# Second attention of a transformer block: scores in four row groups and four banks, softmax in pieces of 616, projection one pair later

## What is computed

```python
q = proj(query, Wq, bq); k = proj(key, Wk, bk); v = proj(value, Wv, bv)     # 16 heads of 16 channels
scores = jnp.einsum('bhqd,bhkd->bhqk', q, k) * scale[None, :, None, None]
scores = scores + _rel_bias(bias_table, tq, tk)[None]
attn = jax.nn.softmax(scores, axis=-1)
out = jnp.einsum('bhqk,bhkd->bhqd', attn, v)
out = out.transpose(0, 2, 1, 3).reshape(b, tq, DIM) @ Wo + bo
x = x + jnp.tanh(g_xattn[1]) * out
```

## Time and profile before

| | us |
|---|---|
| median of 3 runs | 486.8 (486.63 to 487.26) |
| profiled execution, first to last instruction | 485.3 |
| second attention, about | 218 to 361 |
| TensorE busy over the span | 434.0 (89%) |
| VectorE, ScalarE, POOL busy | 334.4, 258.2, 128.3 |
| mean granted TensorE clock, share of full | 0.959 |

### The profile page before, as it was taken

How to read it: one execution, slowest core, us unless ns; L and a number is a source line. 1 busy time by engine, 2 the same in 40 slices (tenths; PEclk the granted TensorE clock), 3 DMA queues, 4 the chain that set the end, 5 groups by cost and what they waited for, 6 DMA issues and landing times.

```text
span 485.3 us, 7506 instructions
## 1 busy us (share of the span) xinstructions
PE 434.0 (89%) x2308; PEld 300.7 (62%) x2309; DVE 334.4 (69%) x732; ACT 258.2 (53%) x453; POOL 128.3 (26%) x143
## 2 busy tenths in 40 slices
PE   8998999999975079999899999999896799999993
PEld 7878544444451078788576577766575467676762
DVE  4999973489998999655667776766827355555562
ACT  3563655599989934323656566655651343332310
POOL 6423262000002504210870000100011754543222
PEclk9999999999985579999999999999998999999998
DMA  8900000000010040000991000000008321221000
GB/s 255 249 3 0 3 2 0 0 0 0 0 58 1 0 105 1 0 0 18 386 407 57 1 1 1 2 0 0 1 20 243 87 78 49 71 51 48 14 30 1
DMA packets 27421, 27.20 MB, mean 56 GB/s; under 512 B 11611, under 2 KB 23586, under 8 KB 27139
## 3 DMA queue, kind: packets, MB, share of 16 engines
q1 hardware_dynamic: 25187, 21.73, 14.5%
q0 software_dynamic: 2208, 5.14, 3.6%
HBM read 22.63 MB, written 5.15 MB: 57 GB/s over the span
## 4 chain that ended last, share of the span: by engine, by line
PE 60%; DVE 17%; issue 3%; ACT 3%; DMA 3%; POOL 2%; DVEq 1%; ACTq 0%; POOLq 0%
PE bank L1661 49%; PE bank L1947 4%; PE bank L1705 3%; DVE big_g L478 2%; DVE big_g L1387 2%; DVE amP L1361 2%; PE bank L2143 2%; DMA token_rows<-x_rows 2%; ACT big_u L760 2%; PE bank L1965 2%; DVE amZ L1297 1%; DVE amU L1303 1%; DVE mx L1482 1%; DVE big_g L1483 1%; PE bank L1973 1%
## 5 line engine op out<-in xcount | busy, mean ns | idle before, releaser
L1661 PE MATMUL bank<-yT,ffn_w 128*128 (+1 forms) x192 | 83.0, 593 | 0.0
L760 ACT ACTIVATE big_u<-bank 77x512 f32<-77x512 f32 (+3 forms) x102 | 56.3, 583 | 34.8 <-PE bank L1947 24.3
L1661 PEld LDWEIGHTS bank<-yT,ffn_w 128*128 128x128 f32 x192 | 36.2, 190 | 44.8 <-issue 43.1
L1661 PE MATMUL bank<-ffn_w,big_u 128*128 128x256 f32 x192 | 42.6, 380 | 0.8 <-ACT big_u L760 0.8
L984 ACT ACTIVATE big_g<-big_g 128x308 f32<-128x308 f32 x64 | 29.0, 456 | 26.1 <-DVE big_g L1483 25.6
L1661 PE MATMUL bank<-k_blockdiag,big_g 128*128 128x308 f32 x128 | 40.2, 430 | 2.5 <-DVE big_g L1483 2.2
L1661 PE MATMUL bank<-big_g,yT 128*128 x92 | 41.8, 595 | 0.6 <-ACT yT L760 0.6
L1059 ACT ACTIVATE yT<-yT 128x512 f32<-128x512 f32 x23 | 14.5, 630 | 52.1 <-DVE yT L1616 52.1
L1661 PE MATMUL bank<-big_u,yT 128*128 x184 | 41.8, 380 | 0.2 <-DVE yT L1630 0.2
L1661 PEld LDWEIGHTS bank<-ffn_w,big_u 128*128 128x128 f32 x192 | 36.2, 190 | 6.0 <-ACT big_u L760 0.9
L1661 PEld LDWEIGHTS bank<-big_u,yT 128*128 128x128 f32 x184 | 34.1, 190 | 5.0 <-issue 0.9
(11 more groups left out here) (293 smaller groups left out, 845.8 us busy)
## 6 DMA issues: line engine op xcount, KB each, us to landing
big_g<-in_L_ffn_W SPq DMA_DIRECT2D x1, 4096.0 KB, 13.5
big_u<-in_L_ffn_W SPq DMA_DIRECT2D x1, 4096.0 KB, 24.5
...
```

Of the source, the lines that this page charges most:

```text
L760: act.activation(out_, in_, ACT.Copy, **k).then_inc(done, 1)
L1661: return pe.matmul(out_, lhsT=lhsT, rhs=rhs, start=first, stop=last)
```

## The change

Each pair is now treated in two halves of eight heads (ci = 0, 1) in place of four quarters.

- Scores (`fill`): for each tile and each group r of 32 rows of `qT` and `KBD` one matmul of 32 rows by 154 columns (the two heads whose channels these rows are), into bank r. A fill is eight matmuls: four row groups for two tiles, side by side in banks 0 to 3 (`quad`). A fill waits until both tiles of the fill before have been read.
- Softmax (`unit`): maximum and subtraction over four banks at once, 616 elements, per tile and half; the exponential in pieces of 616 too.
- The weights' transposes of one tile use banks 6 and 7 in turn; heads are two blocks of eight matmuls into bank 5, the transposes back into banks 5 and 6, queries and projection both in bank 4.
- The projection of pair t - 4, no longer of t - 2, is issued during pair t, and so are its residual and moments. Two projections (pairs 12 and 14) are left for the tail.
- The last four down tiles, and the late layer norm tiles, get other banks and places around pair 0.
- All hardware loops of the stage are written out. `oT` gets memory of its own, and `pT` another order of its quarters (`PLACES`).

```diff
@@ -26,6 +26,10 @@
 HQ = 4
...
+HC = H // CH
+HCK = HC * KEYS
+RG = 4
+RK = HCK // RG
...
 FJ = F // P
@@ -244,8 +248,9 @@
         def sem(name):
             return ctx.enter_context(nc.semaphore(name))
-        bank = [ctx.enter_context(nc.psum_tensor(f"bank{i}", [P, 512], F32)) for i in range(8)]
-        pb = [b[:, :] for b in bank]
+        quad = ctx.enter_context(nc.psum_tensor("quad", [P, 4, 512], F32))
+        bank = [ctx.enter_context(nc.psum_tensor(f"bank{i}", [P, 512], F32)) for i in range(4, 8)]
+        pb = [quad[:, i, :] for i in range(4)] + [b[:, :] for b in bank]
         rows_d = nc.dram_tensor("token_rows", [NT * P, ROW], F32).ap()
@@ -393,9 +398,9 @@
...
-        oT = part(TMP, 0, [P, NQ, 2 * P])
+        oT = sb("heads_out", [P, NQ, 2 * P])
...
-        mx = sb("mx", [P, 2, HQ])
+        mx = sb("mx", [P, 2, HC])
...
@@ -453,8 +458,8 @@
         ob = part(YW, 3584, [P, 2, D])
...
+        LAST = NT - 2
+        PLACES = (0, 2, 1, 3)
         def position(t):
@@ -967,55 +971,54 @@
...
+            def weightsT(t, ci, u):
+                for k in range(2):
+                    o = PLACES[2 * ci + k] * HQ
+                    copy(pT[:, o:o + HQ, u * P:(u + 1) * P], pb[6 + k][0:KEYS, :].rearrange("k (h p) -> k h p", h=HQ),
+                         s.pT_ps, 2 * (2 * t + 2 * ci + u) + k + 1, s.pT_sb)
+            def heads_out(t, ci):
+                copy(oT[:, 2 * ci:2 * ci + 2, :], pb[5].rearrange("p (a n) -> p a n", a=2), s.oT_ps, t + ci + 1, s.oT_sb)
             def attended(t):
                 act.wait_ge(s.attT_ps, t + 2)
...
+                act.activation(attT, pb[5 if t == LAST else 4].rearrange("p (a n) -> p a n", a=2), ACT.Copy).then_inc(s.attT_sb, 2)
+            def exponents(t, ci, u):
+                e8 = e_[:, u, ci * HCK:(ci + 1) * HCK]
+                act.wait_ge(s.e_sub, 2 * t + 2 * ci + u + 1)
+                act.activation(e8, e8, ACT.Exp).then_inc(s.e_exp, 1)
+            def pair(t):
+                if t:
+                    weightsT(t - 2, 1, 0)
+                    if t >= 4:
+                        attended(t - 4)
                     else:
...
+                        y3_out_late(NQB - 1, 0)
+                    weightsT(t - 2, 1, 1)
+                    if t < 4:
+                        y3_out_late(NQB - 1, 1)
+                exponents(t, 0, 0)
+                if t == 0:
+                    y3_out_late(NQB - 2, 0)
+                    y3_out_late(NQB - 2, 1)
+                exponents(t, 0, 1)
+                if t:
+                    heads_out(t - 2, 1)
+                weightsT(t, 0, 0)
+                weightsT(t, 0, 1)
+                exponents(t, 1, 0)
+                if t < LAST:
+                    queries(t + 2)
+                exponents(t, 1, 1)
+                heads_out(t, 0)
+            for t in range(0, NT, 2):
+                pair(t)
+            weightsT(LAST, 1, 0)
+            attended(LAST - 2)
+            weightsT(LAST, 1, 1)
             def y4T_out(k):
@@ -1026,10 +1029,11 @@
                 copy(lT[:, g, :], pb[(0, 4)[g % 2]][:, 0:P], s.lT_ps, g + 1, s.lT_sb)
             y4T_out(0)
...
+            y4T_out(1)
+            heads_out(LAST, 1)
+            for k in range(2, 5):
                 y4T_out(k)
...
+            attended(LAST)
             y4T_out(5)
             logits_out(0)
             logits_out(1)
@@ -1445,102 +1449,94 @@
             def head_out(t, u):
                 dve.wait_ge(s.o_ps, t + u + 1)
...
+                o = pb[u if t == LAST else 5 + u][:, 0:H * VE].rearrange("p (h d) -> p h d", d=VE)
                 c.link(dve.reciprocal(rd[:, u, :], o[:, :, HD]))
                 dve.tensor_tensor(att[:, u, :].rearrange("p (h d) -> p h d", d=HD), o[:, :, 0:HD],
                                   rd[:, u, :].unsqueeze(2).to_broadcast([P, H, HD]), ALU.mult).then_inc(s.att_sb, 1)
...
+            def residual(t, u):
                 dve.wait_ge(s.wo_ps, t + 2)
...
+                x = X[:, tile_at(t) + u, 0:D]
+                dve.tensor_tensor(x, pb[5 if t == LAST else 4][:, u * D:(u + 1) * D], x, ALU.add).then_inc(s.x3_done, 1)
+            def moments(t):
+                tile = tile_at(t)
                 dve.wait_ge(s.x3_done, t + 2)
                 dve.sem_inc(s.dve_past, 1)
                 for u in range(2):
...
+                    mk = c.mark(dve.bn_stats(stat[:, u, :], X[:, tile + u, 0:D]))
                 dve.wait_ge(s.dve_step, mk)
                 dve.sem_inc(s.dve_past, 1)
                 for u in range(2):
                     mk = c.mark(dve.bn_aggr(mv[:, u, :], stat[:, u, :]))
                 dve.wait_ge(s.dve_step, mk)
...
+                dve.tensor_copy(mv4[:, tile:tile + 2, :], mv[:, 0:2, :]).then_inc(s.mv_d, 2)
+            def unit(t, ci, u):
+                dve.wait_ge(s.s_ps, t + ci + 1)
+                s8 = quad[:, :, u * RK:(u + 1) * RK].rearrange("p r (h k) -> p r h k", k=KEYS)
+                e8 = e_[:, u, ci * HCK:(ci + 1) * HCK].rearrange("p (r h k) -> p r h k", r=RG, k=KEYS)
+                m8 = mx[:, u, :].rearrange("p (r h) -> p r h", r=RG)
+                if t % TB == TB - NEAR:
+                    o = u * HK + ci * HCK
+                    near = BN[:, t // TB, o:o + HCK].rearrange("p (r h k) -> p r h k", r=RG, k=KEYS)
+                    c.link(dve.tensor_tensor(e8, s8, near[:, :, :, ::-1], ALU.add))
+                    s8 = e8
+                c.link(dve.tensor_reduce(m8, s8, AX.X, ALU.max))
+                dve.tensor_tensor(e8, s8, m8.unsqueeze(3).to_broadcast([P, RG, HC // RG, KEYS]),
+                                  ALU.subtract).then_inc(s.e_sub, 1)
             def first_pair():
                 last = NT - 4
...
+                x2(last, pb[5])
+                x2(last + 1, pb[6])
+                unit(0, 0, 0)
+                x2(last + 2, pb[7])
+                unit(0, 0, 1)
+                x2(last + 3, pb[5])
                 stats([rows(last + u) for u in range(4)], s.mv_c, (s.x2_done, NT))
...
+                unit(0, 1, 0)
                 y3_made(NT // 4 - 1)
...
+                unit(0, 1, 1)
+            def pair(t):
+                if t % TB == TB - NEAR:
+                    dve.wait_ge(s.near_sb, 1)
+                unit(t, 0, 0)
+                unit(t, 0, 1)
+                if t >= 4:
                     dve.wait_ge(s.bo_added, 1)
...
+                    residual(t - 4, 0)
+                    residual(t - 4, 1)
+                    moments(t - 4)
+                unit(t, 1, 0)
+                head_out(t - 2, 0)
+                unit(t, 1, 1)
+                head_out(t - 2, 1)
+            first_pair()
+            for t in range(2, NT, 2):
+                pair(t)
+            residual(LAST - 2, 0)
+            residual(LAST - 2, 1)
+            moments(LAST - 2)
             def ln_rows(a, b):
                 dve.tensor_copy(X[:, a:b, RSTD], rstd4[:, a:b])
                 return dve.scalar_tensor_tensor(X[:, a:b, NMR], mv4[:, a:b, 0], -1.0, rstd4[:, a:b],
                                                 ALU.mult, ALU.mult)
...
+            head_out(LAST, 0)
+            head_out(LAST, 1)
             dve.wait_ge(s.rstd_d, 2)
             ln_rows(0, TB)
             ln_rows(TB + NEAR, NT).then_inc(s.ln_row, 1)
...
+            residual(LAST, 0)
+            residual(LAST, 1)
+            moments(LAST)
             dve.wait_ge(s.lg_ps, NT // 4)
             lg = pb[1].rearrange("p (t e) -> p t e", e=32)[:, :, 0:E]
@@ -1929,48 +1923,55 @@
             y3_in(1)
...
+            def fill(t, ci):
+                n = (t // TB * CH + ci) * HC
+                if t + ci:
+                    pe.wait_ge(s.e_sub, 2 * (t + ci))
+                if ci == 0:
+                    pe.wait_ge(s.q_sb, t + 2)
                 for u in range(2):
...
+                    for r in range(RG):
+                        rows_ = slice(r * P // RG, (r + 1) * P // RG)
+                        ins = mm(quad[:, r, u * RK:(u + 1) * RK], qT[rows_, ci, u * P:(u + 1) * P],
+                                 KBD[rows_, n + 2 * r:n + 2 * r + 2, :].rearrange("p h k -> p (h k)"), True, True)
+                ins.then_inc(s.s_ps, 1)
+            def weightsT(t, ci, u):
+                n = 2 * t + 2 * ci + u
+                pe.wait_ge(s.e_exp, n + 1)
+                for k in range(2):
+                    if n:
+                        pe.wait_ge(s.pT_sb, 2 * (n - 1) + k + 1)
+                    if (ci, u, k) == (1, 0, 0) and t:
+                        pe.wait_ge(s.att_sb, t)
                     for h in range(HQ):
...
+                        o = (2 * ci + k) * HQK + h * KEYS
+                        ins = pe.transpose(pb[6 + k][0:KEYS, h * P:(h + 1) * P], e_[:, u, o:o + KEYS], ident[:, :])
                     ins.then_inc(s.pT_ps, 1)
...
+            def heads(t, ci):
+                pe.wait_ge(s.pT_sb, 2 * (2 * t + 2 * ci + 1) + 2)
+                for k in range(2):
+                    for g in range(HQ):
+                        h = (2 * ci + k) * HQ + g
```

(72 more changed lines are left out.)

216 lines of the change are left out of this document (9 added, 207 removed).

## The result

| | before | after |
|---|---|---|
| median (lowest to highest of 4 runs), us | 487.0 (486.6 to 491.9) | 462.2 (460.9 to 462.6) |
| profiled execution; its span, us | 486.8; 485.3 | 460.9; 459.1 |
| ratio, 95% interval | | 0.947 (0.943 to 0.950) |

The change takes about 25 us off. The forecast was 457.0 with a range of 453.5 to 477.5: the mechanism of case A, 5 us short of the time and just outside case A's own range of 454 to 462.

What follows compares the result with a forecast made beforehand. TensorE alone was taken to set the second attention's pace. Start, pairs and tail summed to a stage end of 330.5 for 361.15, 30.6 less; minus 0.8, 29.8; span 455.5, plus 1.5 gives 457.0. Range 453.5 to 477.5.

Steps and rivals of the forecast that it cites:

- case A: The forecast itself: score row groups run side by side, TensorE sets the pace; 457, own range 454 to 462, chance 0.62.
- C: Rival in the score fills: row groups' weight loads go one behind the other, 16 x 0.11 = 1.76 per fill; 477, chance 0.11.
- D: Rival in the score fills: row groups run one behind the other, 2.08 for 0.52 per fill; 482, chance 0.07.
- E: Rival in the score fills: the array runs empty before each next record, 0.28 each, fill 4.5; 521, slower, chance 0.05.
- The fill, 0.67: Score fill on TensorE, start to next start: four rounds of 0.13 = 0.52, plus 0.15 for filling and leaving.
- The ordinary pair, 12.05: TensorE's blocks of one new pair sum to 11.9 us; 0.13 added for places where ScalarE comes last.
- case B: Rival: eviction takes over, fills wait for units to be read, ordinary pairs go to 13.4; 464, chance 0.13.
- Pair 2, 10.8: Second attention's pair 2, which has no projection to issue: 10.8 us.
- Start, near pair: Stage start to pair 2 takes 13.6, gain 5.2; the near-table pair becomes VectorE's, 13.4 us for 17.0.
- The tail, 25.35: Pair 14's start at 305.15 to the last residual at 330.5, with last heads starting at 322.9.
- the 0.8 left for copies: Allowance of 0.8 us in the stage's gain for late copies, cutting 30.6 to 29.8.
- Behind the last residual: Router and experts after the stage: 124.1 us, which the change leaves alone.

Runs made afterwards that it cites:

- halved softmax: The changed kernel with the softmax's maximum and subtraction in pieces of 308 over two banks, four operations per unit: 469.3 us, ratio 0.957.

## Why the prediction was right, and where it was short

**Row groups side by side, A against C, D and E.** Right, and now measured by itself: one group in place of four costs 2.81 us per pair, and that is nearly all of the change's gain within an ordinary pair (3.29). C falls by the weight loads (0.6 us busy for sixteen), D and E by the fill. Case C's 0.11 for a load was read from transposes whose loads have 77 columns (0.87 / 8); the four transposes with loads of 128 columns give the same 0.11 (0.44 / 4).

**The fill, 0.67.** It is 0.73 to 0.74. In the trace's single records of pair 8 the second round's matmuls start 0.235 behind the first, the third and fourth follow at 0.131 each, and the next block 0.240 later: 0.737. So the rounds are the 0.13 forecast, and the term that was too small is the filling and leaving: 0.74 - 4 x 0.131 = 0.21, for the 0.15 taken over from column strips, where heads confirm it (1.00 = 4 x 0.216 + 0.14). The 0.64 that the forecast quotes for the router's block is its duration; from start to start the block takes 0.58, which is 4 x 0.107 + 0.15.

**The ordinary pair, 12.05.** It is 12.31, with no wait of TensorE. The blocks add up to 0.39 more than the 11.92 of the sum: 0.13 in the two fills, 0.06 in each of two blocks of four transposes (0.50 for 0.44), 0.04 in each of two blocks of eight (0.91 for 0.87), 0.07 in the projection (1.89 for 1.82), the rest in hundredths. 0.13 of that had been left for late copies, which don't occur. Prices had been read ahead of one neighbour and used ahead of another; which neighbour costs the 0.04 to 0.07 was not tested. Four pairs make 1.0 us.

**VectorE, and case B.** Unit 1.55 for 1.54, slack 1.05 for 1.0. The halved softmax shows that it hides. B therefore fell in ordinary pairs, and held in the two near pairs, as its row said. The Trainium skill's rule ("TensorEngine Tiling (Array Packing)", PSUM Bottleneck) agrees with the near pair's 1.05 us of idle TensorE and not with the ordinary pair.

**Pair 2, 10.8.** It is 11.45. The second half of the late layer norm transposes lies in it, and behind them the heads wait 0.40 for ScalarE's copies, which stand in one queue with the layer norm's. The forecast had not walked this pair's copies. The other 0.25 is in the prices of the blocks, as in the ordinary pair.

**Start, near pair.** To pair 2 13.33 for 13.6; near pair 13.43 for 13.4.

**The tail, 25.35.** It is 29.22, the step that failed outright. Three terms: the last near unit ends 13.71 behind the start of pair 14 for 13.40 (0.3); the third unit's transposes and the projection's, 0.93 + 0.44, lie behind the wait for the last unit and not ahead of it (1.4); and the clock (2.1). The walk had only the last unit, its exponential and what follows in the queue. It missed that the third unit's block, ahead of them in TensorE's queue, waits for a semaphore that VectorE raises only behind the fourth unit. The forecast gave 0.02 to a clock that falls in the stage and put nothing into the sum for it; it fell for 6.8 us. From the last heads on the tail was as forecast: 335.43 - 327.81 = 7.62 for 7.18 + 0.44.

**The sum.** Against the forecast span of 455.5: start of the stage -0.4 (218.74 for 219.14), start to pair 2 -0.3, pair 2 +0.65, four ordinary pairs +1.05, tail +3.9, the 0.8 left for copies -0.8, behind the last residual -0.4 (123.67 for 124.1): 459.1. The median adds 0.3 around the span and 1.3 by which the profiled execution lies below it: 462.2. The 0.8 was meant for late copies, and what it offset was other things: that much of the total is luck. That the time lies well inside the whole range says little, since the range was drawn to reach case C.

**Behind the last residual** the change does nothing, as forecast: 123.6 for before and for after on the third chip. On the other two chips the same instructions took 127.0 to 130.7 in eight kernels. After, and the kernel with each group's tiles behind each other on the first group's chip, from 20 to 40 us behind the last residual:

```profile
355.40:375.40 20.00, 19.36 (x79) 12.38 (x80) 9.15 (x15) 9.94 (x23) 11.72 (x13) 1.00 0.31 90
```

```profile
356.10:376.10 20.00, 14.93 (x60) 9.17 (x61) 6.71 (x12) 7.48 (x17) 8.96 (x11) 1.00 0.23 61
```

TensorE does 60 instructions there for 79; tokens are gathered by DMA in this stretch. In each of the eight profiles TensorE has an idle gap of 1.3 to 4.1 us, 27 to 30 us behind the last residual; in those of the third chip it has none there. Before wasn't profiled on those chips, but its median is 3 us higher there too. What differs between the chips stays open.
